# Loading, first projections and cross-attention in one block, with inputs laid out by the host

## The reference

```python
x = x + cross_attention(layernorm(x), ctx)          # this change is in here
x = x + block(layernorm(x))                         # self-attention, router, 8 experts

def cross_attention(x, context):                    # x (4, 256, 128), context (4, 512, 256)
    q = heads(x @ Wq) * 64 ** -0.5                  # 16 heads of 64
    k, v = heads(context @ Wk), heads(context @ Wv) # Wkv is (256, 2048)
    k, v = concat(null_k, k), concat(null_v, v)     # one learned extra key and value per head
    out = softmax(q @ k.T) @ v                      # 513 keys
    return layernorm(out @ Wout) * scale + bias
```

## Time and profile before

| | us |
|---|---|
| median of 3 runs (646.16 to 647.5) | 646.84 |
| the profiled execution | 646.28 |
| its span, first to last instruction | 644.2 |
| first product of keys starts on PE | 16.93 |
| last queue of the first block ends, first query starts | 34.8, 35.13 |
| first further key tile (step 0) starts on PE | 44.68 |
| first transposes of probabilities (step 0) | 48.34 |

### The profile page before, as it was taken

One profiled execution on the slowest core, in us unless ns is written; L12 is line 12 of the kernel. 1 busy time (PEld: TensorE's weight loads), 2 busy tenths in 40 slices (PEclk: granted clock), 3 DMA queues, 4 the chain that ended last, 5 costly groups with the idle time before them and its releaser, 6 DMA issues. The chain is left out here.

```text
span 644.2 us, 11036 instructions
## 1 busy us (share of the span) xinstructions
PE 565.5 (88%) x3380; PEld 439.3 (68%) x3380; DVE 491.0 (76%) x1030; ACT 420.2 (65%) x1024; POOL 323.6 (50%) x606
## 2 busy tenths in 40 slices
PE   2969999999999899999988657989886599999996
PEld 1737768777777677787766545656554578888885
DVE  4757877886788587978689526998884479999995
ACT  2538777786768656777677416889883365656653
POOL 1345766785678765787676556366965100000000
...
DMA packets 14394, 13.14 MB, mean 20 GB/s; under 512 B 2049, under 2 KB 13697, under 8 KB 14337
## 3 DMA queue, kind: packets, MB, share of 16 engines
...
q10 hardware_dynamic: 304, 0.03, 0.0%
HBM read 11.92 MB, written 0.52 MB: 19 GB/s over the span
## 5 line engine op out<-in xcount | busy, mean ns | idle before, releaser
L1071 POOL TENSOR_SCALAR attn_probs<-attn_probs,rinv 128x512 f32<-128x512 f32 x128 | 87.6, 698 | 21.1 <-DVE rinv L975 21.1
L848 ACT ACTIVATE attn_probs<-bank,bias 128x512 f32<-128x512 f32 x128 | 87.3, 687 | 12.3 <-DVE bias L968 12.3
L984 DVE TENSOR_TENSOR pT_lo<-bank,pT_hi 128x512 fp32r<-128x512 f32 x128 | 86.7, 679 | 6.7 <-ACT pT_hi L864 5.4
L960 DVE TENSOR_REDUCE neg_max<-bank 128x1 f32<-128x512 f32 x128 | 83.9, 676 | 6.4 <-PE bank L686 6.4
L701 PE MATMUL bank<-ident,attn_probs 128*128 128x128 f32 x512 | 78.3, 282 | 10.2 <-POOL attn_probs L1071 9.3
L701 PEld LDWEIGHTS bank<-ident,attn_probs 128*128 128x128 f32 x512 | 56.1, 141 | 36.1 <-POOL attn_probs L1071 19.6
L864 ACT ACTIVATE pT_hi<-bank 128x512 fp32r<-128x512 f32 x128 | 74.2, 595 | 8.8 <-PE bank L701 8.0
L731 PE MATMUL bank<-pT_hi,vals 128*128 128x256 f32 x256 | 67.0, 294 | 2.2 <-DVE pT_lo L984 1.4
L731 PE MATMUL bank<-pT_lo,vals 128*128 128x256 f32 x256 | 64.9, 286 | 0.0
L1885 ACT ACTIVATE act_hi<-act_f 128x512 fp32r<-128x512 f32 x56 | 35.4, 633 | 43.4 <-DVE act_f L1926 43.3
L731 PEld LDWEIGHTS bank<-pT_hi,vals 128*128 128x128 f32 x256 | 49.4, 193 | 4.5 <-DVE pT_lo L984 2.0
(11 more groups left out here) (311 smaller groups left out, 1603.9 us busy)
## 6 DMA issues: line engine op xcount, KB each, us to landing
ctx_raw<-in_ctx SPq DMA_DIRECT2D x4, 512.0 KB, 4.7
...
x<-in_x SPq DMA_DIRECT2D x1, 512.0 KB, 6.7
wq_raw<-in_L_xattn_Wq SPq DMA_DIRECT2D x1, 512.0 KB, 10.2
wout_raw<-in_L_xattn_Wout SPq DMA_DIRECT2D x1, 512.0 KB, 12.1
```

The lines of the kernel that those rows point to most:

```text
L848: act.activation(probs[:, g % 2, i, t, :], score_bank(G, i)[:, :], ACT.Exp, bias=bias[:, t, h:h + 1], scale=X_SCALE, accum_out=row_sum[:, ...
L960: dve.tensor_reduce(neg_max[:, t, h:h + 1], score_bank(G, i)[:, :], AX_X, ALU.max, negate=True).then_inc(max_s, 1)
L984: dve.tensor_tensor(pT_lo[:, i, 2 * half:2 * half + 2, :], t_bank[half][:, :].rearrange("p (j n) -> p j n", j=2), f(pT_hi[:, i, 2 * half:2 ...
L1071: pool.tensor_scalar(probs[:, g % 2, i, t, :], probs[:, g % 2, i, t, :], rinv[:, t, h:h + 1], 1.0, ALU.mult, ALU.mult).then_inc(p_norm_s, 1)
```

## The change

The block `load_and_split` is gone. Its work stands ahead of the steps in `cross_attention`, as methods of a class `Prologue`, and the steps start at 0: pair 0's queries, scores, exponentials and pair 1's first scores are written out between the first products. The products use two PSUM banks in place of four. The host lays out x and Wout so that one row in memory holds all that goes to one partition, gives the context already turned (all four batches), and adds a turned copy of Wq, from which PE makes `w0` in eight small matmuls. Wkv is loaded and split in five pieces; the first load of x is two token tiles. So the context's transposes on PE are gone, at the start and at steps 3, 11 and 19; there ACT and DVE read the loaded context itself. The rest of x (six tiles) is turned as two units among the products. The remaining null scores and `u` come last on PE before step 0. POOL's three jobs are moved: Wout's low part to step 0, the bias on x to step 2, the self-attention's weights to step 3.

Cut to its core:

```diff
-FIRST = [("c", 0, 0), ("c", 1, 0), ("k", 0, 0), ("k", 1, 0), ("k", 2, 0),
-         ("v", 0, 0), ("v", 0, 1), ("v", 0, 2), ("v", 0, 3), ("k", 3, 0)]
...
+FIRST = [("k", 0, 0), ("k", 1, 0), ("x", 2, 6), ("k", 2, 0), ("v", 0, 0), ("k", 3, 0),
+         ("v", 0, 1), ("v", 0, 2), ("v", 0, 3), ("x", 6, 8)]
+EARLY_HEADS = 4
...
+    def loads(self, sp, dram):
+
+        k = self.k
+        sp.dma_start(k.x[:, 0:QT, :], dram["x_tiles"][:, 0:QT, :]).then_inc(self.x_in, 16)
+        sp.dma_start(k.ctx_raw[:, :, :], dram["ctx_T"][0, :, :, :]).then_inc(k.ctx_in, 16)
+        self.load_piece(sp, dram, KEYS_A)
+        sp.dma_start(self.wq_raw[:, :, :], dram["L0_xattn_Wq"].rearrange("c (h d) -> c h d", h=H)).then_inc(self.wq_in, 16)
+        self.load_piece(sp, dram, KEYS_B)
+        sp.dma_start(self.wqT_raw[:, :, :], dram["wq_T"]).then_inc(self.wqT_in, 16)
+        sp.dma_start(k.x[:, QT:TT, :], dram["x_tiles"][:, QT:TT, :]).then_inc(self.rest_in, 16)
+        for piece in (VALUES_A, KEYS_C, VALUES_B):
+            self.load_piece(sp, dram, piece)
+        sp.dma_start(self.wout_raw[:, :, :], dram["wout_tiles"]).then_inc(self.wout_in, 16)
...
+    def unit(self, pe, n):
+
+        k, (kind, i, t), out = self.k, FIRST[n], self.bank(n)
+        if n >= 2:
+            pe.wait_ge(k.first_lo, n - 1)
+        if kind == "x":
+            pe.wait_ge(self.xn_ready, 2)
+            for tile in range(i, t):
+                last = pe.transpose(out[:, (tile - i) * P:(tile - i + 1) * P], self.xn[:, tile, :], k.ident[:, :])
+        else:
+            piece = VALUES_A if kind == "v" else KEYS_A if i < 2 else KEYS_B
+            pe.wait_ge(self.c0_lo, 1)
+            pe.wait_ge(self.piece_lo, SPLIT_ORDER.index(piece) + 1)
+            last = project(pe, k, kind, i, t, out)
+        last.then_inc(k.first_ps, 1)
...
+    def null_queries(self, pe):
+
+        pe.wait_ge(self.diag_set, 1)
+        pe.wait_ge(self.wqT_in, 16)
+        for p in range(HP):
+            last = pe.matmul(self.pW0, self.wqT_raw[:, p, :], self.nk_diag[:, p, :], start=p == 0, stop=p == HP - 1)
+        last.then_inc(self.null_ps, 1)
...
-                if b >= 2:
-                    sp.wait_ge(c_ps, (b - 1) * CT)
-                sp.dma_start(k.ctx_raw[:, :, :], dram["ctx_2048"][b, :, :].rearrange("(t p) c -> p t c", p=P)).then_inc(k.ctx_in, 16)
+                sp.wait_ge(*((c_lo_s, (b - 1) * CT) if b >= 2 else (first.c0_lo, 1)))
...
-            def context_unit(g, i):
-                b = context_at(g)
-                if b is None:
-                    return
-                if i == 0:
-                    pe.wait_ge(k.ctx_in, (b + 1) * 16)
-                    pe.wait_ge(q_lo_s, g + 3)
-                else:
-                    pe.wait_ge(c_lo_s, (b - 1) * CT + 1)
-                project(pe, k, "c", i, 0, unit_bank).then_inc(c_ps, 1)
...
+            first.first_tokens(pe)
+            first.unit(pe, 0)
+            project_q(0)
+            first.unit(pe, 1)
+            first.null_queries(pe)
+            pe.wait_ge(k.first_lo, 1)
+            scores(0, 0)
+            first.null_scores(pe, range(QT), (first.x0_hi, 1)).then_inc(first.null_ps, 1)
+            project_q(1)
+            scores(0, 1)
+            for n in (2, 3, 4):
+                first.unit(pe, n)
+            scores(1, 0)
+            for n in range(5, len(FIRST)):
+                first.unit(pe, n)
+            pe.wait_ge(first.s0_s, 1)
+            first.null_scores(pe, range(QT, TT), (k.first_hi, len(FIRST)))
+            first.null_outputs(pe)
             for s in STEPS:
                 transpose_probs(s - 1, 1, 1)
...
                 project_q(s + 2)
                 weighted_values(s, 0)
-                context_unit(s, 0)
                 scores(s + 2, 0)
-                context_unit(s, 1)
...
+            first.small_loads(act, dram)
+            act.wait_ge(k.ctx_in, 16)
+            act.activation(k.cT_hi[:, :, :], k.ctx_raw[:, :, :], ACT.Copy).then_inc(first.c0_hi, 1)
+            first.piece_head(act, KEYS_A)
+            act.wait_ge(first.x0_ps, 1)
+            act.activation(k.xnT_hi[:, 0:N], first.side[:, 0:N], ACT.Copy)
+            act.activation(first.xnT[:, 0:N], first.side[:, 0:N], ACT.Copy).then_inc(first.x0_hi, 1)
+            act.wait_ge(first.wq_in, 16)
+            act.activation(k.wq_hi[:, 0:EARLY_HEADS, :], first.wq_raw[:, 0:EARLY_HEADS, :], ACT.Copy).then_inc(first.wq_hi_s, 1)
+            first.piece_head(act, KEYS_B)
+            first.head(act, 0)
+            q_head(0)
...
+            early = slice(0, QT)
+            dve.wait_ge(first.x_in, 16)
+            token_stats(dve, range(QT), lambda t: k.x[:, t, :], first.stats, first.mean_var, first.x_var, 2)
+            first.normal(dve, range(QT), 1)
+            dve.wait_ge(first.c0_hi, 1)
+            dve.tensor_tensor(k.cT_lo[:, :, :], k.ctx_raw[:, :, :], f(k.cT_hi[:, :, :]), ALU.subtract).then_inc(first.c0_lo, 1)
+            first.piece_tail(dve, KEYS_A)
+            dve.wait_ge(first.x0_hi, 1)
+            dve.tensor_tensor(k.xnT_lo[:, 0:N], first.side[:, 0:N], f(k.xnT_hi[:, 0:N]), ALU.subtract).then_inc(first.x0_lo, 1)
+            dve.wait_ge(first.wq_hi_s, 1)
+            dve.tensor_tensor(k.wq_lo[:, 0:EARLY_HEADS, :], first.wq_raw[:, 0:EARLY_HEADS, :], f(k.wq_hi[:, 0:EARLY_HEADS, :]), ALU.subtract)\
+                .then_inc(first.wqA_lo, 1)
+            first.diagonals(dve)
+            first.tail(dve, 0)
+            q_tail(0)
+            first.piece_tail(dve, KEYS_B)
+            dve.wait_ge(first.rest_in, 16)
+            token_stats(dve, range(QT, TT), lambda t: k.x[:, t, :], first.stats, first.mean_var, first.x_var, 4)
+            first.tail(dve, 1)
+            dve.wait_ge(first.null_ps, 1)
+            dve.tensor_copy(first.w0[:, :], first.pW0).then_inc(first.w0_ready, 1)
+            maximum(0, 0, 0)
+            maximum(0, 0, 1)
+            first.null_shift(dve, early, (first.null_ps, 2))
+            dve.wait_ge(first.s0_s, 1)
+            shift(0, 0)
+            first.normal(dve, range(QT, TT), 2)
+            q_tail(1)
+            first.piece_tail(dve, VALUES_A)
+            maximum(0, 1, 0)
+            maximum(0, 1, 1)
+            shift(0, 1)
+            inverse_sum(0, 0)
+            first.tail(dve, 2)
+            first.tail(dve, 3)
+            inverse_sum(0, 1)
+            first.piece_tail(dve, KEYS_C)
+            first.tail(dve, 4)
+            maximum(1, 0, 0)
+            maximum(1, 0, 1)
+            shift(1, 0)
+            for n in range(5, len(FIRST)):
+                first.tail(dve, n)
+                if n == 6:
+                    first.piece_tail(dve, VALUES_B)
+            first.null_shift(dve, slice(QT, TT), (first.u_hi_s, 1))
+            dve.tensor_tensor(k.u_lo[:, :], first.pU, f(k.u_hi[:, :]), ALU.subtract).then_inc(first.u_lo_s, 1)
...
+            def output_weights():
+                pool.wait_ge(first.wout_hi_s, 1)
+                pool.tensor_tensor(k.wout_lo[:, :, :], first.wout_raw[:, :, :], f(k.wout_hi[:, :, :]), ALU.subtract).then_inc(first.wout_lo_s, 1)
+
+            def residual_bias():
+                pool.wait_ge(bias_in, 16)
+                pool.wait_ge(first.xn_ready, 2)
+                pool.tensor_tensor(k.x1[:, :, :], k.x1[:, :, :], over_tiles(k.bias_row), ALU.add).then_inc(k.x_bias_s, 1)
...
+            def self_weights():
+                pool.wait_ge(w_in, 4 * 16)
+                linked(pool, k, pool.tensor_tensor(k.wqkv[:, :, :], k.wqkv[:, :, :],
+                                                   k.ln1_col[:, :].unsqueeze(2).broadcast_to([P, FH + 2 * KV, HD]), ALU.mult))
+                wqkv = k.wqkv[:, :, :].rearrange("p h d -> p (h d)")
+                linked(pool, k, pool.tensor_scalar(k.wqkv_hi[:, :], wqkv, 1.0, 1.0, ALU.mult, ALU.mult))
+                pool.tensor_tensor(k.wqkv_lo[:, :], wqkv, f(k.wqkv_hi[:, :]), ALU.subtract)
...
+                if s == 0:
+                    output_weights()
+                if s == 2:
+                    residual_bias()
+                if s == 3:
+                    self_weights()
                 whole_sum(s + 1, 0)
...
+    laid_out = {
+        "x_tiles": np.asarray(inputs["x"]).reshape(B, QT, P, D).transpose(2, 0, 1, 3).reshape(P, TT, D),
+        "ctx_T": np.asarray(inputs["ctx_2048"]).reshape(B, M, CT, P).transpose(0, 3, 2, 1),
+        "wq_T": np.asarray(inputs["L0_xattn_Wq"]).T.reshape(HP, P, D).transpose(1, 0, 2),
+        "wout_tiles": np.asarray(inputs["L0_xattn_Wout"]).reshape(HP, P, D).transpose(1, 0, 2),
+    }
```

More of the change, by code:

```diff
@@ L78, in project @@
 def project(pe, k, kind, i, t, out):
-    if kind == "c":
-        for tile in range(KT):
-            last = pe.transpose(out[:, tile * P:(tile + 1) * P], k.ctx_raw[:, tile, i * P:(i + 1) * P], k.ident[:, :])
-        return last
     n = 0
@@ L236, in _ @@
[L236 to L251 removed]
+        self.k = k
@@ L531, in cross_attention @@
         probs = sb("attn_probs", [P, 2, 2, QT, M])
+        banks = [bank(f"bank{i}") for i in range(8)]
```

(5 more changed lines are left out.)

373 lines of the change are left out of this document (180 added, 193 removed).

## The result

The changed kernel takes 642.13 us (median of six executions, 640.24 to 644.23) against 647.71 of the kernel before (646.16 to 648.28; 646.84 was the median of the first three of its six): ratio 0.9917, interval 0.9896 to 0.9938, so 5.6 us less. Run again on another chip it took 640.61 against 645.75 (0.992, 0.990 to 0.994). The forecast was 639.8 in 635.5 to 644.5. The execution shown here took 644.23 us, the longest of the six; its mean granted clock was 0.956.

The account below looks back on a forecast made before the run. Steps are bound by PE's work, so gains ahead of the first transposes (48.34) reach the end; DVE's queue bounds the units. From 646.28: -7.4 earlier transposes, +0.7 clock, +1.2 POOL's jobs, -1.0 contexts give 639.8, range 635.5 to 644.5.

Parts of the forecast that it names:

- loads: Before product 0: small first load lands near 3.5, others follow at 411 KB per us; product 0 at about 7.9, not 16.93.
- clock: Before step 0: one stretch at the lower clock in PE's gaps between 17 and 25 costs 0.7 us; bounds 0 and 2.5.
- contexts: Context steps: without eight transposes on PE each saves 0.35 us, -1.0 for three; bounds 0 and -3.6.
- the prediction's own signs: Wrong would be: transposes after 44, first product after 11, units of 2.8 us or more, steps growing over 2 us in sum.
- 1.5 us later than by rows: First product, by the skill table's 240 GB/s for the first 896 KB, against the profile rows' estimate; time would be 640.3.
- First bias: Pair 0's first bias on DVE must wait for POOL, busy until 18.2 with Wq's low part; forecast at 18.3.
- Units: Units 2 to 9 before step 0: DVE's queue bounds; eight units from 19.9 to 35.7, 15.8 us or 2.0 each.
- slower rival: Units 2 to 9 run one behind the other, eight take 25.6 us instead of 15.8: 649.6; chance 0.06.
- Null work: After the last unit: six null scores (1.4) and u (1.85) alone on PE, 3.3 us, up to 38.6.
- POOL's jobs: Steps 2 and 3: bias on x costs about 0.9 us, self-attention's weights 0.3, together +1.2; bounds 0 and 4.1.

## Why the prediction was right, and where it was off

The direction and the range held, and so did the mechanism up to step 0: with the pair put behind the units again the gain is gone (646.86). 642.13 lies 2.3 us over the 639.8. The medians are 5.6 and 5.1 apart, near the forecast 6.5. That is in part luck, for in the profiled executions three terms (loads, clock, contexts) missed by over a microsecond each, all to the slow side. There the change is worth 644.23 - 646.28 = -2.05: first transposes -3.84 instead of -6.7, steps 0 to 31 +1.71 instead of +0.2, the rest +0.08. The profiled executions were the longest of the changed kernel both times, and that of the kernel before was among its shortest; what a middle execution of the changed kernel looks like, no profile shows. By the prediction's own signs, transposes after 44 would have been wrong, and they came at 44.50 in the first profile and at 43.95 in the second.

The 2.85 us by which the first transposes came late (44.50 against 40.95 + 0.7) come apart in full: product 0 1.44, from there to unit 2 0.1 (12.11 against 12.0), and from unit 2 to step 0 1.3 (23.05 against 21.05 + 0.7), which is the clock.

*Loads.* "The others follow at 411 KB per us: 4.7, 5.4 ..." failed. x was there at 3.2 and the context near 5.1, but the first keys piece only at 7.8 instead of 5.4. A load is there when the last of its parts is, and the parts were 2.3 us apart (5.50 to 7.81); I had taken the sum of bytes over the rate. Product 0 came 1.44 us late; about 1.0 of the piece's 2.4 was slack, as the forecast had DVE busy with the context until 7.2. By the Trainium skill, "DMA: Bandwidth & Descriptors", section "Bandwidth", whose table gives small loads less than full rate, I had estimated 1.5 us later than by rows. By that rule this profile agrees in the start of product 0, 9.34 against 7.9, though the piece itself was later, the start moved between 8.29 and 9.63 with the same loads, and part of it was the 4-byte packets.

*First bias.* Forecast 18.3, begun at 18.23, held by POOL until 19.77. Right in mechanism; 18.3 was meant as its end, and that came as late as product 0 did. The hold is worth 0.9 us, measured by moving it away. The Trainium skill, "SBUF — State Buffer", section "SBUF: two separate sides", says that POOL and DVE share a pair of ports that one instruction keeps to its end, also a DVE instruction with two SBUF inputs. The trace agrees in three places on DVE, with 2.46 instead of 0.84, 1.54 instead of 0.16 and 2.42 instead of 1.22. On POOL's side it is less plain: the normalise takes 1.21 instead of 0.70, and ends 0.5 us after DVE's subtraction, less than it takes alone.

*Units.* From 21.45 to the last low part at 37.54 the eight units (six products and two turns of x) took 16.1 us, forecast 15.8: right. The slower rival needed 2.8 us a unit.

*Null work and clock.* The null work stood alone on PE as I said. The clock term was +0.7. In the execution with 10.2 us at the lower clock it cost 1.9 against one of the same code with 3.4, which took 21.11 from unit 2 to step 0, and the run that kept PE busy, with none, took 21.06. The forecast's sum without the clock is 21.05. So the term was nearer its upper bound of 2.5 there.

*Steps.* POOL's jobs cost 0.90 and 0.32, forecast 0.9 and 0.3: right. The contexts failed: -1.0 was forecast, with nothing as the upper bound. Against the kernel before the six steps around them are 1.1 us longer, 0.3 of it POOL's, so some 0.8; against the same kernel with its contexts on PE they cost 1.0. I had written that "the two copies and subtractions stay" and not looked at what they read. The subtraction went from PSUM to two SBUF operands, and so to the kind of hold that I used for POOL's jobs two sentences before.
